# Decoder of two layers on one Trainium2 core: another order of each group's work on TensorE in the causal self heads

## The reference, cut to what matters

```python
def _L1_attn_ref(x, w_qkv, w_out):
    B, T, D_IN, D_OUT, NH = (4, 512, 256, 256, 16)
    HD = D_OUT // NH
    SCALE = 1.0 / float(np.sqrt(HD))
    qkv = jnp.einsum('btd,ed->bte', x, w_qkv).reshape(b, t, 3, NH, HD)
    q, k, v = jnp.moveaxis(qkv, 2, 0)
    scores = jnp.einsum('bqhd,bkhd->bhqk', q, k) * SCALE
    causal_bias = (1.0 - jnp.tril(jnp.ones((t, t), dtype=x.dtype))) * -10000.0
    attn = jax.nn.softmax(scores + causal_bias, axis=-1)
    out = jnp.einsum('bhqk,bkhd->bqhd', attn, v).reshape(b, t, D_OUT)
    return jnp.einsum('btd,ed->bte', out, w_out)
```

## Time and profile before

| what | value |
|---|---|
| three runs | 1813.83, 1824.99, 1825.43 us; median 1824.99 |
| the profiled execution | 1820.29 us, with a span of 1818.4 us |
| mean granted clock of TensorE | 0.959 of 2.4 GHz |
| busy over the span | PE 92%, DVE 75%, ACT 57%, POOL 38% |
| self heads, from the first maxima to the last turn | 781.3 to 1003.4 us |
| cross heads | about 1145 to 1660 us |

### The profile page before, as it was taken

How to read it: one execution, slowest core, us unless ns; L and a number is a source line. 1 busy time by engine, 2 the same in 40 slices (tenths; PEclk the granted TensorE clock), 3 DMA queues, 4 the chain that set the end, 5 groups by cost and what they waited for, 6 DMA issues and landing times. The chain is left out here.

```text
span 1818.4 us, 35284 instructions
## 1 busy us (share of the span) xinstructions
PE 1664.5 (92%) x13824; PEld 912.9 (50%) x13824; DVE 1363.4 (75%) x2337; ACT 1043.8 (57%) x1748; POOL 686.0 (38%) x771
## 2 busy tenths in 40 slices
PE   8998999989999998879999887799999999999996
PEld 4786677668888886423333654122222222223564
DVE  4535888756666665868885779999999999995664
ACT  4322655436566554337777333277888888887542
POOL 2783777024445443423340343215412121111453
PEclk9999999989999998969999999599999999999998
DMA  6163999777877763621110466221201011000001
GB/s 222 55 221 125 318 314 326 241 268 300 310 293 293 290 263 124 205 69 29 37 35 5 152 202 195 49 65 54 73 20 38 20 27 30 19 20 1 24 12 35
DMA packets 111693, 244.55 MB, mean 134 GB/s; under 512 B 27890, under 2 KB 80630, under 8 KB 107908
## 3 DMA queue, kind: packets, MB, share of 16 engines
q1 hardware_dynamic: 84712, 204.56, 32.1%
q0 software_dynamic: 24176, 35.12, 7.3%
q10 hardware_dynamic: 2640, 2.62, 0.4%
HBM read 180.27 MB, written 61.38 MB: 133 GB/s over the span
## 5 line engine op out<-in xcount | busy, mean ns | idle before, releaser
L2205 DVE TENSOR_REDUCE Eh_maxima<-Eh_max 128x2 f32<-128x802 f32 x512 | 474.8, 987 | 21.6 <-PE Eh_max L2077 16.7
L2193 ACT ACTIVATE Eh_probs<-Eh_pair 128x1024 f32<-128x1024 f32 (+1 forms) x288 | 287.5, 998 | 112.5 <-PE Eh_pair L2124 112.4
L2077 PE MATMUL Eh_max<-Eh_KS,Eh_QS 49*128 49x401 f16 x1024 | 197.7, 357 | 44.9 <-DVE Eh_maxima L2205 41.1
L2146 PE MATMUL Eh_av_ps<-Eh_probs,E_V 128*17 128x512 f32 (+1 forms) x1664 | 223.0, 609 | 0.0
L1537 PE MATMUL C_y<-C_x_high,C_W 128*128 128x256 f16 (+1 forms) x1536 | 214.8, 253 | 8.9 <-ACT C_gate L1597 7.4
L1537 PE MATMUL C_y<-C_x_low,C_W 128*128 128x256 f16 (+1 forms) x768 | 180.5, 252 | 0.0
L2193 ACT ACTIVATE Eh_probs<-Eh_single 128x512 f32<-128x512 f32 x272 | 161.7, 594 | 28.0 <-PE Eh_single L2124 27.8
L2205 DVE TENSOR_REDUCE Dh_maxima<-Dh_max 128x2 f32<-128x1024 f32 x128 | 152.0, 1221 | 31.9 <-PE Dh_max L2093 30.7
L1915 POOL DMA_DIRECT2D Eh_KS<-E_kd x64 | 37.1, 579 | 354.0 <-PE Eh_pair L2124 349.1
L2077 PEld LDWEIGHTS Eh_max<-Eh_KS,Eh_QS 49*128 49x128 f16 x1024 | 50.5, 94 | 233.1 <-DVE Eh_maxima L2205 198.2
L1537 PEld LDWEIGHTS C_y<-C_x_high,C_W 128*128 128x128 f16 x1536 | 139.0, 98 | 22.3 <-ACT C_gate L1597 9.6
(11 more groups left out here) (463 smaller groups left out, 3481.2 us busy)
## 6 DMA issues: line engine op xcount, KB each, us to landing
C_W<-w_split SPq DMA_DIRECT2D x24, 3072.0 KB
w_split<-B_w_parts SPq DMA_DIRECT2D x24, 768.0 KB, 8.1
Eh_KS<-E_kd POOLq DMA_DIRECT2D x64, 150.1 KB, 3.3
C_tail<-in_expert_tail_dram SPq DMA_DIRECT2D x24, 384.0 KB, 8.4
B_places<-in_w_experts_dram SPq DMA_DIRECT2D x10, 768.0 KB, 6.8
early_more<-in_w_experts_dram SPq DMA_DIRECT2D x8, 768.0 KB, 9.4
early_ctxT<-in_ctxT_dram SPq DMA_DIRECT2D x6, 800.5 KB, 6.0
early_ctxT<-in_w_experts_dram SPq DMA_DIRECT2D x6, 768.0 KB
```

Source lines behind the costliest of these rows:

```text
L2077: last = self.nc.tensor.matmul(bank[:, a, 0:self.cw], self.QS[r, slot, p, qt * P:(qt + 1) * P], self.KS[r, slot, p, k0:k0 + self.cw], star ...
L2146: last = self.nc.tensor.matmul(self.av_ps[u * STRIP:u * STRIP + VW, :], self.V[0:r, kt, unit * VW:(unit + 1) * VW], self.probs[0:r, self.b ...
L2193: self.nc.scalar.activation(dst, src, ACT.Exp, scale=1.0 / SCORE).then_inc(self.exp_done, 1)
L2205: self.nc.vector.tensor_reduce(self.maxima[:, g % 2, :, p * TPB + qt, c], self.max_ps[n % 2][:, :, 0:self.cw], AX_X, ALU.max).then_inc(sel ...
```

## The change

Only the string changes. Counted by kind, a group had 5 S, 6 B, 2 M, 4 V, R and T; now it has 3 S, 8 B, no M, 4 V, R and T. Every product, reduction and exponential is still made, in the same number.

```diff
         run_heads(nc, Heads(own, nc, "Dh", S, places, V, ATT, (ident, ident_half, ident_score), tri, 6, 4,
-                            "S V B S T B B V B S R V B B V S S M M"))
+                            "B S B V B T B V B R B V B S B V S"))
```

## The result

| | before | changed |
|---|---|---|
| median of five executions | 1818.74 us | 1885.26 us (1872.04 to 1887.17) |
| ratio to before | | 1.035, 95% interval 1.0324 to 1.0376 |
| profiled execution, span | 1820.29, 1818.4 us | 1872.04, 1870.2 us |
| granted clock of the executions | 0.959 (profiled) | 0.953 (profiled), 0.942 to 0.946 (the other four) |
| self heads, first maxima to the start of the last T | 781.3 to 1002.0 us | 782.6 to 1051.6 us |

The change makes the kernel 3.5% slower, on the side that was forecast. The point forecast, 1863 us, is too low by 22 us against the median and by 9 us against the profiled execution; the median lies 1 us above the upper end of the range. The trace shows which term is off.

What follows compares the result with a forecast made beforehand. TensorE was taken to bound the kernel, with almost no waits before. Waits less saved work (37.7 us over 13 groups), 0.5, 1.2 and 1.8 at the ends and 2 for the clock gave +43.2, 1863 us; whole range 1851 to 1884.

Steps and rivals of the forecast that it cites:

- What bounds the kernel: Middle of the changed stage: TensorE sets the pace, with only 0.3 us of a 12.40 us group spent waiting before.
- the walk: Item-by-item timing of one new group on TensorE: 11.63 us of work plus 3.67 of waits, 15.30 us against 12.40.
- Work saved, 0.48 us per group: Per group on TensorE: two score and two maxima items become two joined items, 0.48 us less work.
- The five waits: TensorE waits added per group: three for ACT (0.67, 0.25, 0.90 us) and two for DVE (0.63, 1.22 us).
- The ends: Stage's start and end: +0.5 us in the first group, +1.2 for a later clock rise, +1.8 in the last two groups.
- The range: Forecast's own range for the kernel time: 1853 to 1873 us, from 30 to 53 us more; whole range 1851 to 1884.
- The clock in the middle: Middle groups, up to 4.93 us between value strips: a clock fall in one of ten of 14 groups, +2 us.
- The recorded sign of being wrong: Middle of the stage: forecast wrong if the clock is below 0.95 or a group takes less than 14.5 us.
- The first one: Rival: the clock falls in nearly every group of the stage, costing 22 us in place of 2, 1883 us; chance 0.14.
- Fewer of the waits bite: Rival: both waits for DVE in a group are absent, 24 us less, 1839 us; chance 0.05.
- The saving wins: Rival: banks come free before TensorE returns, so only the joining's saving is left, 6 us less, 1814 us; chance 0.03.

Runs made afterwards that it cites:

- Experiment 4: Kernel before, with only its last two score items and two maxima items joined into two joined items, all else in place: 1826.28 us, ratio 1.0023.
- experiment 6: Kernel before, with added products that nothing reads from the first maxima to the first value strip: 1824.68 us, ratio 1.0032.
- experiment 2: Changed kernel with a maxima product repeated three times during the idle time at each group's start only: 1864.78 us; changed kernel rerun on the same chip: 1880.44 us.

## Why the prediction was right, and where it was off

- **What bounds the kernel.** Right: the group's length followed TensorE's items and their waits in each of eight orders or fills, within 0.2 us of the walk (12.76 for 12.7, 14.69 and 14.58 for 14.6, 15.36 for 15.30, 12.07 for 11.9).
- **Work saved, 0.48 us per group.** Experiment 4 has the same joins; with the wait of 0.8 us that they bare it costs 0.37, so they save about what was said.
- **The five waits.** By distances: op 2 0.68 (said 0.67), behind T 936.61 - 935.27 - 0.71 = 0.63 (0.63), behind R 940.24 - 938.31 - 0.71 = 1.22 (1.22), op 9 0.25 (0.25), op 0 945.73 - 944.36 - 0.48 = 0.89 (0.90). The group is 2.97 us longer for 2.90. DVE is busy 71% where less than 70% was said.
- **The ends.** 5.5 us over the first two groups and the last two with the tail, where 0.5, 1.2, 1.8 and one group of 2.9 make 6.4. The second group costs 2.3 and not 4.1: probably since half-rate items leave ACT more time, so that there is less to wait for. It was not tested. The 1.2 us rested on the clock rising only once value strips run. It did rise later, at 820.8 us in place of 816.7, but experiment 6 has it at 1.00 before any strip, so the reason was wrong and the direction partly luck.
- **The range.** 30 us above 1820.3 is 1850, so the forecast's own lower bound of 1853 does not follow from it. Nothing measured hangs on that bound.
- **The clock in the middle: the term that failed in size.** It stood as "one in ten of 14 groups gives +2 us". The profiled execution had five falls, 7.2 us, and the others, by their clock, about one in each group. The step took the share of falls, 3 of 30, from a stage whose groups take 32.4 us (1285.69 to 1318.11) and counted the distance between strips alone. Here a group takes 15.36 us, and both idle stretches (0.7 and 0.9 us) stand in that distance once in each. With one of them filled the same distance of 4.97 us had no fall in the middle (experiment 2), so the distance was the wrong thing to count. That the idle stretches are needed for the falls is shown; why they bring five in one execution and, by the clock, some 13 in another is not. The recorded sign of being wrong, a clock below 0.95 in the middle, was narrowly not met in the trace (0.96 from 831.02 to 1022.52 us); with a fall in every group it would be about 0.90.
- **The rivals.** The first one, the clock falling in nearly every group, gave 1883 us at a chance of 0.14. Four of five executions, 1882.23 to 1887.17 us, lie at its time, though their falls are read from their mean clock alone; only the one with the trace, 1872.04 us, lies near the forecast. It should have had the larger chance. That the direction and the size of the waits came out is the walk's merit; that the median lies only 1 us above the range is owed to this rival, whose 22 us had set its upper end. The Trainium skill ("TensorE: Matmul & The Clock Gate", "A second HAM failure mode: psum-queue depth-cycling") has small gaps between groups of matmuls as a cause of such swings of the clock. This case agrees: idle stretches of 0.7 and 0.9 us were enough, and the falls went when one was filled. "Fewer of the waits bite" fell, since both waits for DVE are there. "The saving wins" fell: the waits sum to 3.67 us in a group, not to less than 0.48.

## What to carry to other kernels

Before reordering a tuned engine, write down for each shared bank the time from an item's end to its release (here 1.15 us for a pair's exponential, 1.42 for a reduction) and walk the new order against it: items on one bank need that much other work between them, and a saving by joining is small beside one wait bared. Then look at where the new idle stretches stand. Two waits that fall between the same two dense strips can cost a fall of TensorE's clock on top of themselves, and a spread of executions with the mean clock is the sign of it. If a wait can't be covered with useful work, a repeat of the next product into its own free bank cost nothing here at full clock and held it; at half clock it lengthened a group (18.76 us in place of 16.21).

## What the runs showed of the hardware that was not expected

- Repeating a product while waiting made the kernel faster: 1862.55 us with five more pairs of 512-column matmuls per group, against 1880 to 1885 without.
- At nearly equal idle share, one trace each: 14.58 us groups with six falls, 14.69 us groups with none.
- The same waits in the same places had a fall in five groups in succession and none in the next six, in both traces of the changed kernel.
- The clock was 0.53 over 18 us with TensorE's rows busy 17.96 of 18.00 us, where full-array matmuls of 256 columns stood among the items (experiment 6).
- The profiled execution had the highest mean clock in both sets of the changed kernel (0.953 against 0.942 to 0.946, 0.956 against 0.945 to 0.951). One trace alone would have put the median 13 us too low.
